# The skip of a chunked recurrence: from four diagonal matmuls on TensorE to a product and a sum on VectorE

## The chip, the cores and the metric

One core of one Trainium2 chip runs the whole kernel. The metric is the device time of one execution in microseconds (us), the median of three runs. A second, profiled execution left the trace from which all rows below are taken.

## What is computed

The reference is a two-layer graph network over N = 4096 nodes of width 256, all in float32. Only the first layer matters here. It adds a graph product to x (4096x4096 weights made from the adjacency matrix by exponentials, times a message matrix), and then a recurrence block:

```
x = x + weights(adj) @ (layernorm(x) @ W + B)
x = x + mamba2(layernorm(x))

# inside mamba2, for 8 heads of 64 channels, t = time step
Y = Y_diag + Y_off + xh * D[:, None]      # D: one number per head, the "skip"
Y = Y * silu(z)
Y = Y * rsqrt(mean(Y * Y)) * norm_w
out = (Y @ W_out) @ W_lin + b_lin
```

`xh * D` is the skip: the convolved input of a channel times its head's D. The second layer (another graph product with a scan, then a mixture of experts) is not touched by the change.

## The kernel before

The 4096 steps are cut into 8 blocks of 512 (`NB`, `TB`), and each block into 4 chunks of 128 steps. The **first stage** of the kernel runs, for every block ib, three streams that are interleaved in one program order per engine: `ssd(ib)` is the recurrence of block ib, `pre_a(ib + 1)` makes the inputs of the next block (norm, projections, convolution, gates), and `product_a(ib + 2)` is the graph product of the block after that. The order is written out as a list (`order_a`, made by `braid`), from which every engine takes its steps. Nothing is scheduled at run time: an engine that waits keeps all that stands behind it waiting too.

Blocks 0 to 5 have a graph product whose weights must be prepared (`product_a`, matmuls of L535). ScalarE takes a logarithm and two exponentials of each tile of `raw`, and VectorE makes two passes over it, L966 and L971 (128x1024 each, two tiles at a time, each with both inputs in SBUF). L535 waits for L971. In blocks 6 and 7 the filling work is the second layer's graph product (L558), whose matrix is used as it is loaded, without preparation.

In a chunk, `inner(s)` turns the chunk's x into rows with four transposes (L610) into a PSUM bank `X`; VectorE makes `xdt` (x times dt, L1066), `bn` (L1069) and `cbm` (L1071) from it; GpSimd makes `rdA` (L1860), `xdec` (L1868, from xdt) and the masked `E` (L1873). `outer(s)` lets TensorE multiply the state h0 (L638, bank `Yo`), make the new state (L643, bank `St`), and sum in bank `Y` first the skip (L648: four 128x128 matmuls with a diagonal matrix of D, `diagD`) and then the in-chunk part (L654: eight matmuls of 64 columns). VectorE takes `tmp` = Yo times a decay (L1082), h0 = hd + St (L1087), tmp += Y (L1091) and z = tmp * z (L1094). GpSimd's `hd` (L1885) decays h0 for the next chunk.

Beside these, the prediction speaks of `xc` (L1011 on VectorE, the last step of pre_a's norm, for which the sixteen small matmuls of L576 wait), of L1049 (the gate's product, behind a tanh on ScalarE), of the transposes L677 behind VectorE's L1104, and of `Wc` (L1132), which is made once in the message stage, the first 45 us, from the matmuls of L712.

Of the kernel before, what the change touches and what calls it, by code (L numbers as in the profile page):

```python
# [9 lines left out]
ALU = mybir.AluOpType  # L10
# [4 lines left out]
NB = N // TB  # L15
# [88 lines left out]
def build(nc, t):  # L104
    with ExitStack() as ctx:
        sems = {}

        def S(name):
            if name not in sems:
                sems[name] = ctx.enter_context(nc.semaphore(name))  # L110
            return sems[name]

        def sb(c, name, shape, dt=F32):
            return c.enter_context(nc.sbuf_tensor(name, shape, dt))
# [28 lines left out]
        diagD = sb(cA, "diagD", [128, 4, 128])  # L143
# [16 lines left out]
        bns = [sb(cA, f"bn{i}", [128, 64]) for i in range(2)]  # L160
        cbm = sb(cA, "cbm", [128, 128])
# [64 lines left out]
        ring_a, ring_b = Ring(PS[2:5], 6 * NB // 2), Ring(PS[5:8], 6 * NB // 2 + 4)  # L226
# [5 lines left out]
        def message_use(ib, i):  # L232
            if ib % 2:
                return ring_b.use(ib // 2 * 6 + (4 if ib > 1 else 0) + i)
            return ring_a.use(ib // 2 * 6 + i)
# [243 lines left out]
        def _(e):  # L479
# [120 lines left out]
            def ssd(ib):  # L600
# [24 lines left out]
                def outer(s):  # L625
# [19 lines left out]
                    w.wait_ge(S("setup"), 7)  # L645
                    w.wait_ge(Y.evac, Y.n - 1)
                    for m in range(4):
                        e.matmul(Y.ps[:, m * 128:(m + 1) * 128], cc[:, m, ts_], diagD[:, m, :], start=m == 0, stop=False,  # L648
                                 skip_group_check=True)
# [3 lines left out]
                    for h in range(8):  # L653
                        i = e.matmul(Y.ps[:, h * 64:(h + 1) * 64], Es[:, h, :], xd[:, h * 64:(h + 1) * 64], start=False,  # L654
                                     stop=h == 7, skip_group_check=True)
# [49 lines left out]
            for i in range(NB // 2):  # L705
                if i == 1:
                    w.wait_ge(S("d_Wo"), 32)
                    for m in range(4):
                        b = combined_use(m)
                        w.wait_ge(b.evac, b.n - 1)  # L710
                        for k in range(2):
                            x = e.matmul(b.ps[:, 0:256], YT[:, k, m * 128:(m + 1) * 128], Wlin[:, k, :],  # L712
                                         start=k == 0, stop=k == 1)
                        x.then_inc(b.full, 1)
                a, b = messages(2 * i), messages(2 * i + 1)
                follow(order_msg[i], a=a, b=b, p=p)
                rest(a)
                rest(b)
# [213 lines left out]
        def _(e):  # L932
# [10 lines left out]
            for m in range(4):  # L943
                e.tensor_scalar(diagD[:, m, :], ident, col("D0", m), None, ALU.mult).then_inc(S("setup"), 1)
# [107 lines left out]
            def ssd(ib):  # L1052
# [3 lines left out]
                def inner(s):  # L1056
# [8 lines left out]
                    w.wait_ge(S("xdec"), c - 1)  # L1065
                    e.tensor_tensor(heads(xd[:, :]), heads(X.ps[:, :]), dt[:, 8 * s:8 * s + 8, None].broadcast_to([128, 8, 64]),  # L1066
# [7 lines left out]
                def outer(s):  # L1074
# [8 lines left out]
                                    ALU.mult).then_inc(Yo.evac, 1)  # L1083
                    yield
# [5 lines left out]
                    w.wait_ge(Yo.evac, Yo.n)  # L1090
# [36 lines left out]
            for i in range(NB // 2):  # L1127
                if i == 1:
                    for m in range(4):
                        b = combined_use(m)  # L1130
                        w.wait_ge(b.full, b.n)
                        e.tensor_scalar(Wc[:, m, :], b.ps[:, 0:256], col("nw", m), None, ALU.mult).then_inc(b.evac, 1)  # L1132
                a, b = messages(2 * i), messages(2 * i + 1)
                follow(order_msg[i], a=a, b=b, p=p)
                rest(a)
                rest(b)
# [863 lines left out]
```

## Time and profile before

| | |
|---|---|
| runs | 2886.9 us median (2885.34 to 2891.23, three runs) |
| profiled execution | 2887.87 us, of which the span of its instructions is 2885.8 us |
| TensorE busy | 2505.6 us (87% of the span) |
| VectorE busy | 2119.0 us (73%) |
| ScalarE, GpSimd busy | 1348.4 us (47%), 961.7 us (33%) |
| mean granted TensorE clock | 0.937 |
| first stage with chunks | about 260 to 1273 us |

Busy time counts a matmul's whole passage through the array, so that a busy TensorE isn't one at its peak. VectorE's 73% is a mean over stages: it is highest in the second layer's scan, behind the stage that is changed.

### The profile page before, as it was taken

The numbers are of one execution on the slowest core, as the hardware profiler recorded it, in microseconds if no ns is written. First come the engines' busy times: TensorE is split into PE (matmuls) and PEld (weight loads), VectorE is DVE, ScalarE is ACT, GpSimd is POOL, SyncE is SP. The second block draws the span as 40 slices with busy tenths as digits, with TensorE's granted clock in tenths as the row PEclk, the third lists the DMA queues.
The fourth block names the chain that finished last, engine by engine and source line by source line (L and its number), as shares of the span: only waits on it lengthen the run. The fifth ranks groups of instructions, "written<-read, shape, count | busy, mean of one in ns | idle before, by whom it ended". The sixth has DMA issues, their size and how long they took to land.

```text
span 2885.8 us, 24290 instructions
## 1 busy us (share of the span) xinstructions
PE 2505.6 (87%) x8262; PEld 1277.1 (44%) x8262; DVE 2119.0 (73%) x2426; ACT 1348.4 (47%) x1935; POOL 961.7 (33%) x723
## 2 busy tenths in 40 slices
PE   7998999999999999988888888888888876765997
PEld 3443444444444444443434343434434343443775
DVE  4665666666667664326999899999999999895564
ACT  4565656565646553214444434434353444552332
POOL 0002232313131313304455554645455464670000
PEclk9998999999999999999999999998999978777999
DMA  4222222222222231123323232322323110102021
GB/s 177 91 88 66 66 83 65 79 71 71 77 73 68 71 104 43 51 83 111 94 83 103 73 109 73 102 80 88 99 84 105 56 50 16 51 31 95 30 66 37
DMA packets 68412, 221.03 MB, mean 77 GB/s; under 512 B 7570, under 2 KB 7826, under 8 KB 67906
## 3 DMA queue, kind: packets, MB, share of 16 engines
q1 hardware_dynamic: 64082, 204.00, 22.4%
q0 software_dynamic: 3664, 14.45, 1.3%
q8 instruction: 66, 1.08, 0.2%
q10 hardware_dynamic: 544, 1.05, 0.1%
q14 instruction: 56, 0.46, 0.1%
HBM read 199.28 MB, written 20.19 MB: 76 GB/s over the span
## 4 chain that ended last, share of the span: by engine, by line
PE 51%; DVE 27%; issue 14%; ACT 6%; POOL 1%; DMA 1%; DVEq 0%; SPq 0%; ACTq 0%; POOLq 0%
PE ps L535 13%; DVE h L1265 9%; DVE acc L1239 7%; PE ps L558 5%; ACT th L1432 2%; PE ps L807 2%; PE ps L654 2%; PE ps L686 2%; PE ps L585 2%; PE ps L587 1%; PE ps L621 1%; PE ps L638 1%; PE ps L643 1%; DVE u L1182 1%; DVE wgt L966 1%
## 5 line engine op out<-in xcount | busy, mean ns | idle before, releaser
L1935 POOL TENSOR_TENSOR dB<-du,bc 128x512 f32<-128x512 f32 x512 | 649.3, 1273 | 559.2 <-DVE h L1265 556.4
L1265 DVE TENSOR_TENSOR_SCAN h<-ps,hst,dB 128x512 f32<-128x512 f32 x512 | 649.3, 1273 | 13.7 <-POOL dB L1935 6.6
L1432 ACT ACTIVATE ps<-dt,cols 128x512 f32<-128x512 f32 x512 | 350.9, 688 | 442.5 <-DVE h L1265 438.3
L535 PE MATMUL ps<-wgt,msg 128*128 128x512 f32 x1024 | 530.7, 621 | 23.0 <-DVE wgt L971 22.6
L558 PE MATMUL ps<-raw,msg 128*128 128x512 f32 x1024 | 543.4, 623 | 3.0 <-DMA msg<-tmp_m 3.0
L807 PE MATMUL ps<-consts,h 128*128 128x128 f32 x2048 | 353.5, 302 | 211.2 <-DVE acc L1239 196.9
L807 PEld LDWEIGHTS ps<-consts,h 128*128 128x128 f32 x2048 | 263.2, 153 | 531.9 <-DVE acc L1239 368.1
L1239 DVE SCALAR_TENSOR_TENSOR acc<-ps,Ct,acc 128x512 f32<-128x512 f32 x450 | 326.7, 726 | 8.9 <-PE ps L807 8.9
L535 PEld LDWEIGHTS ps<-wgt,msg 128*128 128x128 f32 x1024 | 184.2, 194 | 254.8 <-issue 200.7
L1432 ACT ACTIVATE wgt<-wgt 128x1024 f32<-128x1024 f32 x256 | 258.1, 1047 | 38.2 <-DVE wgt L966 35.7
L558 PEld LDWEIGHTS ps<-raw,msg 128*128 128x128 f32 x1024 | 176.5, 199 | 127.8 <-issue 127.0
L966 DVE SCALAR_TENSOR_TENSOR wgt<-wgt 128x1024 f32<-128x1024 f32 x128 | 176.4, 1418 | 69.5 <-ACT wgt L1432 69.5
L971 DVE SCALAR_TENSOR_TENSOR wgt<-raw,wgt 128x1024 f32<-128x1024 f32 x128 | 163.6, 1318 | 17.6 <-ACT wgt L1432 17.3
L1432 ACT ACTIVATE wgt<-raw 128x1024 f32<-128x1024 f32 x128 | 127.8, 1046 | 0.6 <-DMA raw<-in_adjT 0.3
L1430 ACT ACT_TABLE_LOAD x81 | 103.9, 1283 | 43.6 <-DVE u L1182 13.7
L1873 POOL TENSOR_TENSOR E<-E,cbm 128x1024 f32<-128x1024 f32 x32 | 81.6, 2551 | 112.5 <-ACT E L1432 107.1
L1845 POOL COPY xbc<-xbc 128x12 f32<-128x12 f32 x8 | 11.9, 1482 | 318.5 <-DVE cc L1036 318.5
L1036 DVE SCALAR_TENSOR_TENSOR cc<-xbc,cols,cc 128x512 f32<-128x512 f32 (+1 forms) x144 | 112.3, 780 | 3.5
L1901 POOL DMA_DIRECT2D tmp_x<-xb x8 | 5.5, 690 | 288.7 <-DVE xb L1114 288.7
L1868 POOL TENSOR_TENSOR xdec<-xdt,ecd 128x512 f32<-128x512 f32 x32 | 33.3, 1042 | 195.0 <-DVE xdt L1066 195.0
L1433 ACT ACTIVATE tmp<-z 128x512 f32<-128x512 f32 x32 | 20.2, 630 | 167.0 <-DVE z L1094 167.0
L1432 ACT ACTIVATE g<-ps,b 128x512 f32<-128x512 f32 x64 | 42.4, 686 | 111.8 <-PE ps L887 109.3
(273 smaller groups left out, 3682.9 us busy)
## 6 DMA issues: line engine op xcount, KB each, us to landing
raw<-in_adjT SPq DMA_DIRECT2D x256, 512.0 KB, 3.6
bc<-tmp_bc SPq DMA_DIRECT2D x64, 512.0 KB, 4.8
xb<-in_xT POOLq DMA_DIRECT2D x8, 512.0 KB, 4.1
tmp_x<-xb POOLq DMA_DIRECT2D x8, 512.0 KB, 3.1
x<-tmp_x SPq DMA_DIRECT2D x8, 512.0 KB, 4.6
tmp_x<-x SPq DMA_DIRECT2D x8, 512.0 KB, 3.5
tmp_xn<-x SPq DMA_DIRECT2D x8, 512.0 KB, 3.6
raw<-tmp_xn SPq DMA_DIRECT2D x8, 512.0 KB, 4.1
```

The source lines that it names most:

```text
L535: x = e.matmul(P[d][:, :], msg[:, j, d * 128:(d + 1) * 128], wgt[g % NW][:, l, :], start=j == 0, stop=j == NJ - 1)
L558: x = e.matmul(P[d][:, :], msg[:, j, d * 128:(d + 1) * 128], raw[g % 4][:, l, :], start=j == 0, stop=j == NJ - 1)
L807: i = e.transpose(b.ps[:, m * 128:(m + 1) * 128], hr[n % 3][:, m, s * 128:(s + 1) * 128], ident)
L966: e.scalar_tensor_tensor(wgt[i % NW][:, :, :], wgt[i % NW][:, :, :], -2.0, wgt[i % NW][:, :, :], ALU.add, ALU.mult).then_inc(S("q"), 1)
L971: e.scalar_tensor_tensor(wgt[i % NW][:, :, :], raw[i % 4][:, :, :], 1.0, wgt[i % NW][:, :, :], ALU.is_lt, ALU.mult).then_inc(S("wgt"), 1)
L1036: e.scalar_tensor_tensor(c, xbc[0:wd, m, k:k + TB], col("cw0", 4 * m + k)[0:wd, :], c, ALU.mult, ALU.add).then_inc(S("conv"), 1)
L1239: e.scalar_tensor_tensor(acc[:, s, :], b.ps[:, :], c, acc[:, s, :], ALU.mult, ALU.add).then_inc(b.evac, 1)
L1265: e.tensor_tensor_scan(hr[n % 3][:, m, :], PS[4 + k % 2].t[:, :], dBr[k % 4][:, :], hst[:, n % 16, m:m + 1], ALU.mult, ALU.add).then_inc(S ...
L1430: e.preload_act_table_set(need)
L1432: return e.activation(out, in_, func, bias=bias, scale=scale)
L1873: e.tensor_tensor(E[s % 2][:, :, :], E[s % 2][:, :, :], cbm[:, None, :].broadcast_to([128, 8, 128]), ALU.mult).then_inc(S("M"), 1)
L1935: e.tensor_tensor(dBr[k % 4][:, :], du[:, m, :], bcr[i % 3][:, n % 2, :], ALU.mult).then_inc(S("dB"), 1)
```

## The change

The skip leaves TensorE. VectorE multiplies X, while it is in PSUM, by a row of D that stands in all 128 partitions (`Dbc`), into a new buffer `skip`, and adds that to `tmp` later on. The four matmuls of a chunk go. `Dbc` is made once: the four diagonal blocks that `diagD` held are written into `skips[0]`, one matmul with a matrix of ones sums them over the partitions, and VectorE copies the sum out of PSUM.

```
-        diagD = sb(cA, "diagD", [128, 4, 128])
+        Dbc = sb(cA, "Dbc", [128, 512])
...
+        skips = [sb(cA, f"skip{i}", [128, 512]) for i in range(2)]
...
@@ TensorE, outer(s)
-                    w.wait_ge(S("setup"), 7)
                     w.wait_ge(Y.evac, Y.n - 1)
-                    for m in range(4):
-                        e.matmul(Y.ps[:, m * 128:(m + 1) * 128], cc[:, m, ts_], diagD[:, m, :], start=m == 0, stop=False,
-                                 skip_group_check=True)
                     yield
...
-                        i = e.matmul(Y.ps[:, h * 64:(h + 1) * 64], Es[:, h, :], xd[:, h * 64:(h + 1) * 64], start=False,
+                        i = e.matmul(Y.ps[:, h * 64:(h + 1) * 64], Es[:, h, :], xd[:, h * 64:(h + 1) * 64], start=h == 0,
...
@@ TensorE, message stage, behind L712
+                    b = combined_use(4)
+                    w.wait_ge(S("setup"), 7)
+                    w.wait_ge(b.evac, b.n - 1)
+                    e.matmul(b.ps[:, :], one, skips[0][:, :], start=True, stop=True).then_inc(b.full, 1)
...
@@ VectorE, start
-                e.tensor_scalar(diagD[:, m, :], ident, col("D0", m), None, ALU.mult).then_inc(S("setup"), 1)
+                e.tensor_scalar(skips[0][:, m * 128:(m + 1) * 128], ident, col("D0", m), None, ALU.mult).then_inc(S("setup"), 1)
...
@@ VectorE, inner(s)
                     w.wait_ge(S("xdec"), c - 1)
+                    w.wait_ge(combined_use(4).evac, combined_use(4).n)
+                    e.tensor_tensor(skips[s % 2][:, :], X.ps[:, :], Dbc[:, :], ALU.mult).then_inc(S("skip"), 1)
                     e.tensor_tensor(heads(xd[:, :]), heads(X.ps[:, :]), dt[:, 8 * s:8 * s + 8, None].broadcast_to([128, 8, 64]),
                                     ALU.mult).then_inc(X.evac, 1)
...
@@ VectorE, outer(s)
                     e.tensor_tensor(heads(tmp[:, :]), heads(Yo.ps[:, :]), ecd[:, 0, s, :, None].broadcast_to([128, 8, 64]),
                                     ALU.mult).then_inc(Yo.evac, 1)
+                    w.wait_ge(S("skip"), c + 1)
+                    w.wait_ge(Yo.evac, Yo.n)
+                    e.tensor_tensor(tmp[:, :], tmp[:, :], skips[s % 2][:, :], ALU.add).then_inc(S("skipped"), 1)
                     yield
...
                     w.wait_ge(Y.full, Y.n)
-                    w.wait_ge(Yo.evac, Yo.n)
+                    w.wait_ge(S("skipped"), c + 1)
                     e.tensor_tensor(tmp[:, :], tmp[:, :], Y.ps[:, :], ALU.add).then_inc(Y.evac, 1)
...
@@ VectorE, message stage, behind L1132
+                    b = combined_use(4)
+                    w.wait_ge(b.full, b.n)
+                    e.tensor_copy(Dbc[:, :], b.ps[:, :]).then_inc(b.evac, 1)
```

The steps' places in the written order stay, so the two new instructions of a chunk stand directly beside those that they follow. The rows below are the order of the built programs. The first place is VectorE's queue at the start of a block: the first chunk's step, the preparation of weights, the second chunk's step and the norm. Before:

```order
L1066 TENSOR_TENSOR xdt<-ps,sm 128x512
L1069 COPY bn<-ps 128x64
L1071 TENSOR_TENSOR cbm<-ps,consts 128x128
L1008 TENSOR_TENSOR xc<-xb,ps 128x1024
L966 SCALAR_TENSOR_TENSOR wgt<-wgt 128x1024 x2
L1066 TENSOR_TENSOR xdt<-ps,sm 128x512
L1069 COPY bn<-ps 128x64
L1071 TENSOR_TENSOR cbm<-ps,consts 128x128
L1011 TENSOR_TENSOR xc<-xc,rr 128x1024
L971 SCALAR_TENSOR_TENSOR wgt<-raw,wgt 128x1024 x2
```

The same place now (line numbers are those of the changed kernel):

```order
L1068 TENSOR_TENSOR skip<-ps,Dbc 128x512
L1069 TENSOR_TENSOR xdt<-ps,sm 128x512
L1072 COPY bn<-ps 128x64
L1074 TENSOR_TENSOR cbm<-ps,consts 128x128
L1009 TENSOR_TENSOR xc<-xb,ps 128x1024
L967 SCALAR_TENSOR_TENSOR wgt<-wgt 128x1024 x2
L1068 TENSOR_TENSOR skip<-ps,Dbc 128x512
L1069 TENSOR_TENSOR xdt<-ps,sm 128x512
L1072 COPY bn<-ps 128x64
L1074 TENSOR_TENSOR cbm<-ps,consts 128x128
L1012 TENSOR_TENSOR xc<-xc,rr 128x1024
L972 SCALAR_TENSOR_TENSOR wgt<-raw,wgt 128x1024 x2
```

Each chunk's product stands ahead of xdt, and so the second one stands ahead of the norm's last step. The second place is VectorE's queue in the third chunk of a block, from the gate's product to the prepared weights. Before:

```order
L1049 SCALAR_TENSOR_TENSOR cc<-th,cc 128x1024
L966 SCALAR_TENSOR_TENSOR wgt<-wgt 128x1024 x2
L1082 TENSOR_TENSOR tmp<-ps,ecd 128x512
L1087 TENSOR_TENSOR hs<-hd,ps 64x512
L1049 SCALAR_TENSOR_TENSOR z<-sq,z 128x1024
L971 SCALAR_TENSOR_TENSOR wgt<-raw,wgt 128x1024 x2
```

And now:

```order
L1050 SCALAR_TENSOR_TENSOR cc<-th,cc 128x1024
L967 SCALAR_TENSOR_TENSOR wgt<-wgt 128x1024 x2
L1085 TENSOR_TENSOR tmp<-ps,ecd 128x512
L1089 TENSOR_TENSOR tmp<-tmp,skip 128x512
L1093 TENSOR_TENSOR hs<-hd,ps 64x512
L1050 SCALAR_TENSOR_TENSOR z<-sq,z 128x1024
L972 SCALAR_TENSOR_TENSOR wgt<-raw,wgt 128x1024 x2
```

The sum with the skip stands between tmp and the state, ahead of the second pass over the weights.

## Rows read from the trace of the kernel before

**Rows 1.** The page's busy times: us, share of the span, instructions.

```profile
PE 2505.6 (87%) x8262; PEld 1277.1 (44%) x8262; DVE 2119.0 (73%) x2426; ACT 1348.4 (47%) x1935; POOL 961.7 (33%) x723
```

**Rows 2.** Busy time by stretch: PE, PEld, DVE, ACT, POOL, granted clock, DMA.

```profile
547.00:553.00 6.00, 6.00 (x7) 1.29 (x6) 1.96 (x3) 2.58 (x5) 3.92 (x3) 0.51 0.44 137
...
1092.00:1230.00 138.00, 129.71 (x483) 66.47 (x484) 56.01 (x88) 36.60 (x64) 44.76 (x30) 0.99 0.14 42
538.00:674.00 136.00, 131.75 (x411) 61.95 (x410) 91.00 (x105) 81.19 (x105) 35.76 (x22) 0.97 0.23 74
```

**Rows 3.** The chain that ended last, blocks 2 to 4: start, us, what.

```profile
538.03 2.91 DVE wgt L966
540.94 0.60 DVE xdt L1066
...
543.80 1.95 PE ps L576 x16
...
554.13 0.89 PE ps L648 x8
...
599.74 0.88 PE ps L535 x2
...
674.20 2.91 DVE wgt L966
...
811.87 2.91 DVE wgt L966
...
951.26 2.91 DVE wgt L966
```

**Rows 4.** GpSimd and VectorE in time behind L576's release, block 2.

```profile
541.62 1.04 POOL L1868 TENSOR_TENSOR xdec<-xdt,ecd 128x512 f32<-128x512 f32 x1 [1.76 <-DVE xdt L1066]
543.68 3.41 POOL L1873 TENSOR_TENSOR E<-E,cbm 128x1024 f32<-128x1024 f32 x1 [1.02 <-ACT E L1432]
...
541.79 1.95 DVE L1011 TENSOR_TENSOR xc<-xc,rr 128x1024 f32<-128x1024 f32 x1
543.67 1.21 DVE L971 SCALAR_TENSOR_TENSOR wgt<-raw,wgt 128x1024 f32<-128x1024 f32 x1
...
544.80 3.37 DVE L971 SCALAR_TENSOR_TENSOR wgt<-raw,wgt 128x1024 f32<-128x1024 f32 x1
```

**Rows 5.** GpSimd and VectorE in time, third chunk of block 2.

```profile
591.68 2.08 POOL L1885 TENSOR_TENSOR hd<-hs,ecd 64x512 f32<-64x512 f32 x1
597.25 4.23 POOL L1885 TENSOR_TENSOR hd<-hs,ecd 64x512 f32<-64x512 f32 x1 [3.49 <-DVE hs L1087]
...
591.63 1.23 DVE L1049 SCALAR_TENSOR_TENSOR cc<-th,cc 128x1024 f32<-128x1024 f32 x1 [4.32 <-ACT th L1432]
...
592.78 2.07 DVE L966 SCALAR_TENSOR_TENSOR wgt<-wgt 128x1024 f32<-128x1024 f32 x1
...
595.90 0.68 DVE L1082 TENSOR_TENSOR tmp<-ps,ecd 128x512 f32<-128x512 f32 x1
596.50 0.67 DVE L1087 TENSOR_TENSOR hs<-hd,ps 64x512 f32<-64x512 f32 x1
```

**Rows 6.** TensorE's weight loads in block 2 that waited for VectorE.

```profile
565.64 0.30 PEld L535 LDWEIGHTS ps<-wgt,msg 128*128 128x128 f32 x2 [0.83 <-DVE wgt L971]
...
599.49 0.30 PEld L535 LDWEIGHTS ps<-wgt,msg 128*128 128x128 f32 x2 [0.58 <-DVE wgt L971]
613.39 0.42 PEld L677 LDWEIGHTS ps<-consts,z 128*128 128x128 f32 x4 [0.75 <-DVE z L1104]
```

**Rows 7.** VectorE's 128x512 product with both inputs in SBUF, grouped.

```profile
L1094 DVE TENSOR_TENSOR z<-tmp,z 128x512 f32<-128x512 f32 x32 | 23.0, 720 | 1.1
```

**Rows 8.** The chain in block 7, the last skip.

```profile
1227.89 0.89 PE ps L648 x8
```

**Rows 9.** The message stage: the last Wc, and TensorE's first L535.

```profile
38.20 0.48 DVE L1132 TENSOR_SCALAR Wc<-ps,cols 128x256 f32<-128x256 f32 x1 [0.38 <-PE ps L712]
...
42.22 1.22 PE L535 MATMUL ps<-wgt,msg 128*128 128x512 f32 x1 [4.06 <-DVE wgt L971]
```

More of the change, by code:

```diff
@@ L223, in build @@
         lane_b = (ccs[0][:, 2:4, :], ccs[0][:, 4:6, :], th[:, 0, :])
-        ring_a, ring_b = Ring(PS[2:5], 6 * NB // 2), Ring(PS[5:8], 6 * NB // 2 + 4)
+        ring_a, ring_b = Ring(PS[2:5], 6 * NB // 2), Ring(PS[5:8], 6 * NB // 2 + 5)
         prod = [Ring(PS[0:1], 2 * NB + 2), Ring(PS[1:2], 2 * NB)]
@@ L233, in message_use @@
             if ib % 2:
-                return ring_b.use(ib // 2 * 6 + (4 if ib > 1 else 0) + i)
+                return ring_b.use(ib // 2 * 6 + (5 if ib > 1 else 0) + i)
             return ring_a.use(ib // 2 * 6 + i)
```

## The prediction

> **What bounds the kernel now.** The page's busy times [rows 1] come first: TensorE has 87% and VectorE 73% of the span, so work is moved from the busiest engine to the second. Shares over a whole span settle nothing, so the stretches come next [rows 2]. In block 2 (538 to 674 us) TensorE is busy 131.75 of 136 us and VectorE 91.00; in blocks 6 and 7 (1092 to 1230) it is 129.71 of 138 against 56.01. VectorE has room in both. Whether it has room where TensorE waits for it, only the chain of waits tells [rows 3]. It is mostly TensorE, but every block of 0 to 5 begins in the same way: VectorE's L966, then xdt, then the norm's last step (L1011), and only then TensorE's L576. From one L966 to the next is 136.17 us (538.03 to 674.20), 137.67 us, then 139.39 us. Last, I looked at TensorE's weight loads that had to wait [rows 6]: in a block of this kind three of them stand close behind VectorE, at 565.64, 599.49 and 613.39. A block is a sequence of stretches, each bounded by TensorE or by VectorE with next to nothing between them. So I cost the change stretch by stretch.
>
> **What goes, what comes.** A chunk's four diagonal matmuls are one piece of 0.89 us on the chain [rows 3] (eight records of 128 columns take what two of 512 do, 0.88). There are 32 chunks. On VectorE each chunk gains a product and a sum of 128x512. The product reads PSUM and a row, as xdt does, which takes 0.60 us on the chain [rows 3]. It is started back to back, so 0.60 is what it adds. The sum reads two SBUF tiles and waits for the tmp ahead of it; the nearest row is L1094, the same shape with the same kind of wait, 0.72 us [rows 7].
>
> **Blocks 0 to 5.** The five terms, each from the end of the one before, with block 2's times.
>
> *Start of the block, to L576.* The product of the second chunk stands ahead of xdt, on the chain: +0.60. It also moves VectorE against GpSimd. Look at the two engines behind L576 [rows 4]: L971's first pass started at 543.67 and took 1.21, and GpSimd's E asked at 543.68 and took 3.41. The second pass of L971 took 3.37, that is 2.16 longer than the first: it stood still until E was done. So these two engines exclude each other here, and VectorE won by 0.01 us. E hangs on ScalarE and TensorE and stays at 543.68; L1011 and L971 come 0.60 later, at 544.28. E is then the first to ask. Does VectorE keep its place, since L1011 holds it and L971 follows without a gap, or is E let in? Both happen in the third chunk [rows 5]: hd, asked for at 591.68 while L1049 ran, was let in ahead of L966 (2.07 where 1.21 is normal), while hd at 597.25 stood behind three passes of VectorE and took 4.23. In the first case, as in the new one, VectorE's running instruction had itself had to wait for GpSimd (L1011 takes 1.95 with xdec running, and L1049 started while E ran); in the second it had not. I take the first as the nearer. Then E runs from 544.28 for about 2.3, L971's first pass is done near 547.8, and TensorE's L535, which began behind L576 at 545.75 (543.80 and 1.95), begins near 548.1. That is +2.3 in all, 1.7 of it for the lost place. The bounds are +0.6 and +2.3.
>
> In the Trainium skill, "SBUF: State Buffer", section "Who interferes with whom", a VectorE instruction with two SBUF inputs and a GpSimd instruction that reads SBUF lock each other out, and whichever issues first holds the ports for its whole instruction. The trace agrees on the lock (3.37 against 1.21). By its letter E, at 543.68, is ahead of L971, at 544.28, and the sum would take +2.3; but the same rule would have let in hd at 597.25, and it was not let in.
>
> *First skip, to L535 at 565.64.* TensorE loses 0.89. The weights that it waits for there come from L971, which hangs on xdt (on L610's transposes, behind the removed skip). That path also gets 0.89 earlier, but carries the new product: -0.89 + 0.60 = -0.29. The new sum lies in VectorE's wait for L643, over 3 us, and is hidden.
>
> *Second skip.* The path to the next weights runs over L654, L1094 and ScalarE, all of them behind TensorE. The new product comes after these weights and before a wait of 4.32 us for the tanh [rows 5], which covers it; the new sum falls into the wait for L643. -0.89.
>
> *Third skip, to L535 at 599.49.* VectorE has no gap here. From L1049 (591.63) on it runs L966 twice, L1082 (595.90), L1087 (596.50), L1049 again and L971; TensorE's L535 begins at 599.74 [rows 3], 0.25 after the load that waited for L971 [rows 6]. The two paths from the tanh are equal, so TensorE's 0.89 gains nothing, and the sum's 0.72 is added: +0.72. What would cover it is a VectorE that had been idle, and it isn't.
>
> *Fourth skip, to L677.* L677 waited for L1104 [rows 6], which hangs on L1094, L1433 and ScalarE from the weights of 599.49 on. TensorE arrives 0.89 earlier and waits: 0. The last sum lies ahead of a wait for ScalarE.
>
> One block: 2.3 - 0.29 - 0.89 + 0.72 = +1.84. Six blocks: +11.0.
>
> **Blocks 6 and 7.** No weights are prepared, VectorE is idle 60% of the time [rows 2], and all eight skips stand on the chain as TensorE's own (the last one in block 7 [rows 8]). The product and the sum fall into VectorE's waits. 8 x -0.89 = -7.1.
>
> **Message stage.** VectorE's L966 starts at once behind the last Wc (38.20), and TensorE's L535 waited 4.06 us for what follows from it [rows 9]. Now one more matmul (0.88) and one more copy (about 0.6) come before L966, less 0.4 that lay between Wc and L966: +1.1.
>
> **Sum.** 11.0 - 7.1 + 1.1 = +5.0 us. The profiled execution took 2887.87 us with a span of 2885.8, 1.0 above the median of the runs. On the median: 2886.9 + 5.0 = 2891.9, so 2892. A measurement of this kernel tells about 0.2%, 5.8 us, from no change: 2881.1 to 2892.7.
>
> **The rivals.**
> - *VectorE keeps its place before E.* The second hd speaks for it [rows 5]. The block's first term is +0.60, a block +0.14, and the sum 0.8 - 7.1 + 1.1 = -5.2: 2881.7. It ends on the other side, and what decides is whether L971, arriving 0.6 us behind E's request, still starts first. Chance 0.25, of which 0.10 beyond the bound.
> - *TensorE alone is the bound.* If L535's waits were absorbed, all 32 skips would pay: -28.5 + 1.1, 2859.5. Against it stand the three loads that waited [rows 6]. Chance 0.07.
> - *The clock.* Between 547 and 553 TensorE was granted 0.51 of its clock [rows 2], so the 1.2 GHz level, right behind the small matmuls of L576 and the wait for L1011. The change makes that wait longer, and adds one of some 1.6 us at 599. The blocks of 139.39 us have more of it than that of 136.17 us [rows 3]: 3.2 us each. If three more blocks get this, or the stretch gets longer, 5 to 10 us come on top: 2897 to 2902. Against it: how the spells fall differs from block to block already, and they can also get fewer. Chance 0.17.
> - *The change doesn't do what it says.* The program's order shows the matmuls gone and both instructions in place, so this is out.
>
> **How the numbers follow.** My forecast has 0.48, within 2886 to 2898, the spread being the clock's; it lies so close to the bound that I give half of it to slower and half to no difference. With the rivals: faster 0.10 + 0.07 and some for fewer slow spells, 0.20; same 0.24 + 0.14 = 0.38; slower 0.24 + 0.17 and a remainder, 0.42. The range leaves out the bound by TensorE alone and the far end of the clock: 2875 to 2904.
>
> **What the profile after would show.** Right: in blocks 0 to 5 E takes about 2.4 us at that place and no longer 3.41, L971's first pass takes over 3 us, and L535 behind L576 waits for it; the load at the third skip waits some 1.6 us more; the period of a block is near 138 us where it was 136.17; 1092 to 1230 is 7 us shorter. Wrong: E still takes over 3.4 us there (then 2882), the period falls by 3 us (then TensorE alone), or granted clocks in blocks differ by more than the sum. The step that I trust least is E's turn, 10 us of the sum; next the clock.

## The result, and the profile after

The changed kernel took 2903.4 us median (2899.17 to 2904.93, six runs) against 2889.4 us (2885.34 to 2891.23, six runs) for the kernel before on the same chip. The ratio is 1.0048, with a 95% interval of 1.0035 to 1.0060: it is slower by 0.48%, +14.0 us, where +5 us was forecast. The time lies in the range, 0.6 us under its upper end, and outside the stretch that I gave my own case (2886 to 2898).

The page's busy times of the changed kernel, to be held against [rows 1]:

```profile
PE 2501.1 (86%) x8008; PEld 1259.8 (43%) x8008; DVE 2193.0 (76%) x2491; ACT 1348.4 (46%) x1935; POOL 959.8 (33%) x723
```

TensorE has 254 instructions fewer and only 4.5 us less busy time, although the skips alone were 32 x 0.89 = 28.5 us. The rest ran at a lower clock (0.929 on the mean of the span, 0.937 before). The same stretches as in [rows 2], counted from the start of the span, so that the last one lies some 15 us earlier in the work than it did before (columns: PE, PEld, DVE, ACT, POOL, granted clock, DMA):

```profile
547.00:553.00 6.00, 5.18 (x19) 3.58 (x20) 6.00 (x3) 1.35 (x2) 6.00 (x3) 0.60 0.23 60
...
538.00:674.00 136.00, 127.78 (x371) 58.62 (x370) 100.82 (x112) 78.48 (x102) 34.97 (x21) 0.95 0.23 74
1092.00:1230.00 138.00, 125.85 (x373) 58.89 (x372) 66.59 (x96) 39.41 (x65) 44.61 (x29) 0.90 0.17 58
```

VectorE counts as busy for all 6 us behind the norm's last step (1.96 before), most of it in passes that stand still, as the rows below show. In the last two blocks the granted clock is 0.90 where it was 0.99. The chain in block 2, which answers to [rows 3]; the block begins 2.90 us later than it did:

```profile
540.93 2.91 DVE wgt L967
543.84 0.60 DVE skip L1068
544.44 0.56 DVE xdt L1069
...
545.37 1.88 DVE xc L1012
547.24 3.31 DVE wgt L972
...
550.59 2.08 PE ps L536 x2
```

The product stands on the chain with its 0.60, and then a new link: L972, the second pass over the weights, 3.31 us. The two engines in time at this place, as in [rows 4]:

```profile
546.59 2.87 POOL L1882 TENSOR_TENSOR E<-E,cbm 128x1024 f32<-128x1024 f32 x1 [0.43 <-ACT E L1441]
549.42 2.02 POOL L1894 TENSOR_TENSOR hd<-hs,ecd 64x512 f32<-64x512 f32 x1
...
547.16 3.38 DVE L972 SCALAR_TENSOR_TENSOR wgt<-raw,wgt 128x1024 f32<-128x1024 f32 x1
...
550.46 3.91 DVE L972 SCALAR_TENSOR_TENSOR wgt<-raw,wgt 128x1024 f32<-128x1024 f32 x1
```

E is now ahead (2.87 us, 3.41 before) and VectorE's first pass takes 3.38 us instead of 1.21. TensorE's loads that waited, as in [rows 6]; the first is new:

```profile
550.59 0.50 PEld L536 LDWEIGHTS ps<-wgt,msg 128*128 128x128 f32 x2 [0.62 <-DVE wgt L972]
...
570.85 0.30 PEld L536 LDWEIGHTS ps<-wgt,msg 128*128 128x128 f32 x2 [1.43 <-DVE wgt L972]
...
604.60 0.30 PEld L536 LDWEIGHTS ps<-wgt,msg 128*128 128x128 f32 x2 [2.27 <-DVE wgt L972]
...
618.50 0.42 PEld L674 LDWEIGHTS ps<-consts,z 128*128 128x128 f32 x4 [1.64 <-DVE z L1110]
```

From the anchor (538.03 before, 540.93 now) the last three come 2.31, 2.21 and 2.21 us later than before.

**The clock at a block's end.** The last wait of blocks 0 to 4, and of the stretch ahead of block 0, is for VectorE's xb (L996; L997 now). The chain from there, first in the kernel before, at the end of block 2:

```profile
661.34 0.69 DVE xb L996
...
662.71 1.10 PE ps L487 x2
663.81 0.44 PE ps L610 x4
...
664.73 1.05 PE ps L489 x2
665.78 1.72 PE ps L535 x4
```

And in the changed kernel:

```profile
666.43 0.69 DVE xb L997
...
667.82 2.05 PE ps L488 x2
669.86 0.85 PE ps L611 x4
...
671.39 1.06 PE ps L490 x2
672.44 1.72 PE ps L536 x4
```

The same matmuls behind the same wait take twice as long (0.44 and 0.85): they run at 1.2 GHz and not at 2.4 (granted clock 0.50 between 667.82 and 670.71, and 1.00 between 662.71 and 664.25 in the kernel before). From the first of them to the next block's 128x1024 subtraction (L1008, L1009 now) it is 3.1 us in the first case and 4.7 in the second. I call this stretch the tail of the block. Of the six tails behind such a wait two were of the short kind before, and none is in this trace. Block 5 has no such wait, and its tail takes 3.1 us in both.

I count a block from one of these subtractions to the next; block 0 begins with the second. There are eight subtractions, and the last begins at 1077.4 us before and at 1092.7 us now:

```profile
L1008 DVE TENSOR_TENSOR xc<-xb,ps x8: 1220/1222/1222, 152.1 to 1077.4; 128x1024 f32<-128x1024 f32 x8
```

```profile
L1009 DVE TENSOR_TENSOR xc<-xb,ps x8: 1220/1220/1222, 151.7 to 1092.7; 128x1024 f32<-128x1024 f32 x8
```

Up to there the two executions differ by +15.3 us. From there to the end of the span they take 1808.4 and 1808.9 us, +0.5, where 7.1 less was forecast. This rest holds blocks 6 and 7 and also some 1650 us of stages that the change doesn't touch. Blocks 6 and 7 by themselves, from the eighth subtraction to the last product of tmp and z (L1094; L1100 now), end here:

```profile
L1094 DVE TENSOR_TENSOR z<-tmp,z x32: 691/692/821, 284.5 to 1231.3; 128x512 f32<-128x512 f32 x32
```

```profile
L1100 DVE TENSOR_TENSOR z<-tmp,z x32: 691/692/822, 283.2 to 1249.3; 128x512 f32<-128x512 f32 x32
```

That is 153.9 us before and 156.6 now.

### The profile page after: what moved, and what is told of

It reads as the page before. It is cut to its first block, busy times and chain, and to the rows that moved or that the text cites. A ratio compares the mean times of both kernels' runs of the same rounds, so it can differ in the third digit from the quotient of the medians.

```text
span 2901.6 us, 23888 instructions
## 1 busy us (share of the span) xinstructions
PE 2501.1 (86%) x8008; PEld 1259.8 (43%) x8008; DVE 2193.0 (76%) x2491; ACT 1348.4 (46%) x1935; POOL 959.8 (33%) x723
## 4 chain that ended last, share of the span: by engine, by line
PE 46%; DVE 30%; issue 14%; ACT 7%; POOL 1%; DMA 1%; DVEq 0%; SPq 0%; ACTq 0%; POOLq 0%
PE ps L536 11%; DVE h L1274 9%; DVE acc L1248 7%; PE ps L559 5%; ACT th L1441 2%; DVE wgt L972 2%; PE ps L808 2%; DVE wgt L967 2%; PE ps L683 2%; PE ps L622 1%; ACT wgt L1441 1%; PE ps L651 1%; PE ps L588 1%; DVE u L1191 1%; PE ps L586 1%
## 5 line engine op out<-in xcount | busy, mean ns | idle before, releaser
L536 PE MATMUL ps<-wgt,msg 128*128 128x512 f32 x1024 | 530.4, 624 | 39.8 <-DVE wgt L972 39.4
L536 PEld LDWEIGHTS ps<-wgt,msg 128*128 128x128 f32 x1024 | 186.6, 195 | 286.4 <-issue 213.1
L967 DVE SCALAR_TENSOR_TENSOR wgt<-wgt 128x1024 f32<-128x1024 f32 x128 | 174.1, 1400 | 65.8 <-ACT wgt L1441 65.8
L972 DVE SCALAR_TENSOR_TENSOR wgt<-raw,wgt 128x1024 f32<-128x1024 f32 x128 | 179.8, 1445 | 17.6 <-ACT wgt L1441 17.2
L1441 ACT ACTIVATE E<-ps 128x512 f32<-128x512 f32 x64 | 38.1, 595 | 121.6 <-PE ps L622 121.5
```

The costliest lines, as they stand in the source:

```text
L536: x = e.matmul(P[d][:, :], msg[:, j, d * 128:(d + 1) * 128], wgt[g % NW][:, l, :], start=j == 0, stop=j == NJ - 1)
L967: e.scalar_tensor_tensor(wgt[i % NW][:, :, :], wgt[i % NW][:, :, :], -2.0, wgt[i % NW][:, :, :], ALU.add, ALU.mult).then_inc(S("q"), 1)
L972: e.scalar_tensor_tensor(wgt[i % NW][:, :, :], raw[i % 4][:, :, :], 1.0, wgt[i % NW][:, :, :], ALU.is_lt, ALU.mult).then_inc(S("wgt"), 1)
L1441: return e.activation(out, in_, func, bias=bias, scale=scale)
```

## The experiments

All ratios are to the kernel before, run on the same chip. "To the 8th" is the start of the eighth subtraction in the profiled execution (the message stage, the stretch up to block 0, and blocks 0 to 5), and "0 to 5" the part of it from the second subtraction on, the six blocks alone. "Rest" is what follows up to the end of the span, and "6, 7" the part of it that is blocks 6 and 7, up to the start of the last L1094. "Block" is the time from the fourth subtraction (529.6 before) to the first matmul behind the block's last wait, so without the tail. In "product, no sum" and "late and held" this block had an additional stretch at half clock; the next two of "late and held" took 133.20 us. The median and the ratio are of the timed runs, the other columns of one traced execution each. The labels that end in 2 stand for edits whose first run gave no time.

| kernel | median us | ratio (95%) | to the 8th | 0 to 5 | rest | 6, 7 | block |
|---|---|---|---|---|---|---|---|
| before | 2889.4 | 1 | 1077.4 | 823.3 | 1808.4 | 153.9 | 133.07 |
| after | 2903.4 | 1.0048 (1.0035 to 1.0060) | 1092.7 | 841.9 | 1808.9 | 156.6 | 135.27 |
| one-column copy | 2902.2 | 1.0041 (1.0027 to 1.0054) | 1090.6 | 835.8 | 1813.0 | 160.9 | 135.68 |
| no skip at all | 2869.4 | 0.9935 (0.9921 to 0.9948) | 1068.4 | 814.3 | 1803.9 | 148.8 | 131.24 |
| product, no sum | 2892.3 | 1.0014 (1.0005 to 1.0023) | 1089.4 | 835.1 | 1803.5 | 148.6 | 135.02 |
| sum, no product | 2876.6 | 0.9960 (0.9946 to 0.9974) | 1071.8 | 818.4 | 1805.4 | 151.6 | 131.97 |
| after, E held | 2890.9 | 1.0016 (1.0007 to 1.0025) | 1081.2 | 826.2 | 1808.8 | 156.6 | 133.27 |
| before, E held | 2887.0 | 0.9995 (0.9986 to 1.0004) | 1077.5 | 823.3 | 1805.0 | 153.8 | 133.07 |
| product late | 2893.3 | 1.0023 (1.0014 to 1.0032) | 1089.7 | 835.7 | 1802.9 | 148.1 | 135.41 |
| late and held | 2879.3 | 0.9975 (0.9962 to 0.9988) | 1075.6 | 822.0 | 1802.0 | 148.2 | 134.32 |
| two products behind, held | 2876.3 | 0.9961 (0.9947 to 0.9974) | 1064.0 | 812.9 | 1803.4 | 148.5 | 132.02 |

**One column copied** (`tiny`), the kernel before with

```
+                    e.tensor_copy(nudge[:, :], X.ps[:, 0:1]).then_inc(S("nudge"), 1)
                     e.tensor_tensor(heads(xd[:, :]), heads(X.ps[:, :]), dt[:, 8 * s:8 * s + 8, None].broadcast_to([128, 8, 64]),
                                    ALU.mult).then_inc(X.evac, 1)
```

> The kernel before, all of its computation kept, with one more VectorE instruction in each of the 32 chunks: a copy of one column (128x1) from the bank of X, issued between the wait on X and the xdt multiplication, where the changed kernel has its product. It asks whether the delay at the start of a block comes from the product's own 0.6 us or from VectorE losing its place to GpSimd's E. Theory of the hand-over: the small copy is enough for VectorE's first wgt multiplication to come after GpSimd's E has begun; the load of TensorE that waits for wgt starts about 1.7 to 1.9 us later in each of blocks 0 to 5, so 6 x 1.8 = about +11 us (+9 to +13), and in the trace E stands ahead of the wgt multiplication. Rival, sum of durations: each copy costs its own 0.06 to 0.1 us, at most 32 x 0.1 = 3 us, and likely under +1 us, since only the first chunk's copy of a block lies on the path.

Measured: ratio 1.0041, so 12 us, and 14 by the medians (2888.2 for the kernel before beside it). The chunk that the expectation calls a block's first is the one that the prediction counts as its second. The two engines at the start of block 2:

```profile
545.25 0.15 DVE L1067 COPY nudge<-ps 128x1 f32<-128x1 f32 x1
...
546.24 1.95 DVE L1012 TENSOR_TENSOR xc<-xc,rr 128x1024 f32<-128x1024 f32 x1
548.11 3.39 DVE L972 SCALAR_TENSOR_TENSOR wgt<-raw,wgt 128x1024 f32<-128x1024 f32 x1
...
548.07 2.35 POOL L1875 TENSOR_TENSOR E<-E,cbm 128x1024 f32<-128x1024 f32 x1 [0.96 <-ACT E L1434]
...
551.55 0.50 PEld L536 LDWEIGHTS ps<-wgt,msg 128*128 128x128 f32 x2 [1.45 <-DVE wgt L972]
```

The copy adds 0.07 us to the chain. That is enough: L972 asks at 548.11, 0.04 after E, where it was 0.01 ahead of it [rows 4], and takes 3.39 us. TensorE's load waits 1.45 us. Counted from the subtraction, L536 begins 1.41 us later and the block is 2.61 us longer; the difference is half clock, since the matmuls behind the wait stayed at 1.2 GHz for longer. Over the six blocks it makes +12.5 us. Two of them (the two that were 1.6 us longer before, by a slow stretch of their own) grew by only 0.7. Blocks 6 and 7, which prepare no weights, took 7.0 us more in this execution, at a granted clock of 0.94 where it was 0.99; it was the longest of the five. The hand-over is shown; the sum of durations, under 1 us, is refuted.

**No skip at all** (`mm_only`), the kernel before without

```
-                    for m in range(4):
-                        e.matmul(Y.ps[:, m * 128:(m + 1) * 128], cc[:, m, ts_], diagD[:, m, :], start=m == 0, stop=False,
-                                 skip_group_check=True)
```

> The kernel before with its 128 diagonal matmuls left out and nothing put in their place, so the skip D*x is missing from the output. It prices what the change gave back. By the terms of the prediction: per block of 0 to 5 the first skip about -0.3 to -0.9 us and the second -0.89, the third and the fourth 0 (VectorE sets the end there), in blocks 6 and 7 eight times -0.89 = -7.1; in sum -14 to -18 us, about 2872 us. Rival, TensorE alone the bound: all 32 chunks pay 0.89, -28.5 us, about 2861. Rival, the clock: the granted clock falls more often once TensorE has these gaps, and blocks 6 and 7 give back less than 3 us of their 7.1, as in the changed kernel's trace, in sum -8 to -12 us.

Measured: 18.8 us less (2888.2 for the kernel before beside it), a little more than the 14 to 18 expected. In a block the chain is 1.83 us shorter (133.07 to 131.24), just the sum of -0.94 at the first skip and -0.89 at the second, with nothing at the third and fourth. So VectorE, for which the loads wait there, sets the end of the third and fourth chunk, and TensorE is not alone the bound. Of blocks 6 and 7, 5.1 us came back, not 7.1. And of 1.83 per block not all stays: this block's tail took 4.4 us where it was 3.1, and the six blocks together are 9.0 us shorter. The traced execution was the longest of the five, 4.8 us above their median, so the trace doesn't show all of the 18.8.

**The product without the sum** (`no_sum`), the changed kernel with

```
-                    e.tensor_tensor(tmp[:, :], tmp[:, :], skips[s % 2][:, :], ALU.add).then_inc(S("skipped"), 1)
```

> The changed kernel without the second half of its work: the product with the row is made in each chunk, the addition to tmp is not (the skip is missing from the output). Against the changed kernel: if the addition's price sits in the third chunk of blocks 0 to 5 only (0.8 us there, hidden elsewhere), the time falls by 6 x 0.8 = 5 us (4 to 7, the third skip paying nothing more), to about 2898 us, still above the kernel before by about 9 us. Rival, all 32 additions count: 32 x 0.79 = 25 us less. Rival, the addition is hidden everywhere: no change.

**The sum without the product** (`no_product`), the changed kernel with

```
-                    e.tensor_tensor(skips[s % 2][:, :], X.ps[:, :], Dbc[:, :], ALU.mult).then_inc(S("skip"), 1)
-                    e.tensor_tensor(tmp[:, :], tmp[:, :], skips[s % 2][:, :], ALU.add).then_inc(S("skipped"), 1)
+                    e.tensor_tensor(tmp[:, :], tmp[:, :], Dbc[:, :], ALU.add).then_inc(S("skipped"), 1)
```

> The changed kernel without the product with X: the addition stays and adds the spread row Dbc itself (the skip is wrong by the factor x). Against the changed kernel: the load that waits for wgt at the start of a block comes 2.2 us earlier as in the kernel before, with VectorE's wgt multiplication ahead of GpSimd's E again, and the first chunk's xdt 0.6 earlier: 6 x (2.2 to 2.9) = 13 to 17 us less, about 2888 us, and so about the time of the kernel before or 1 to 5 us below it. Rival, the sum of durations: only 0.6 us in a block, 4 to 7 us less, about 2898 us.

Measured: without the sum +0.14%, so 0.34% under the changed kernel, about 10 us, where 5 was expected. The trace confirms the place: in block 2 it is 6.59 us from the gate's product (L1050) to the pass L972 at the third skip, where the changed kernel has 7.39 and the kernel before 6.60, so the sum makes 0.8. The further 5 us are not assigned. The traced executions are 8.7 us apart, 5.4 of it in the rest, but two later executions of the changed kernel differ from its first by 3.2 and 5.8 us there with nothing changed. Without the product the time is 0.40% under the kernel before, so 0.88% or 25 us under the changed one, where 13 to 17 was expected. Its block shows the sum by itself: 131.97 against 131.24 without any skip, +0.73, in place of the 0.72 of the prediction. The product thus makes 3.3 of the changed kernel's 135.27: 1.9 at the start (L536 behind L577), 0.6 ahead of the next xdt, and 0.8 that the clock adds. Blocks 0 to 5 took 818.4 us without the product, 18 to 23 less than in three executions of the changed kernel, so most of the 25 lies where it was expected. Both expectations had the place right and were too small. The clock is the part that block 2 shows; how much of the 10 and 25 us it makes in the timed runs is not shown.

**E held back** (`hold_e2`), the changed kernel with one wait on GpSimd ahead of E:

```
+                    if s == 1 and ib < 6:
+                        w.wait_ge(S("wgt"), 36 + 16 * ib)
                     e.tensor_tensor(E[s % 2][:, :, :], E[s % 2][:, :, :], cbm[:, None, :].broadcast_to([128, 8, 128]),
                                    ALU.mult).then_inc(S("M"), 1)
```

> The changed kernel, all of it, with one more wait: in the chunk beside the anchor of blocks 0 to 5 GpSimd begins its multiplication of E only when VectorE has done the two wgt multiplications that follow there. The order of the kernel before (VectorE ahead of E) is so restored by a semaphore, while the product stays where it is. Theory of the hand-over: the first wgt multiplication takes about 1.2 us again and TensorE's load waits for it no more; of the 2.2 us that a block lost at its start 1.6 come back and the product's 0.6 stays: 6 x 1.6 = about -10 us against the changed kernel (-8 to -13), about 2893 us. Rival, E is what counts: E ends some 2 us later and the Y matmuls, which wait for it, take the delay over: no gain or a loss.

**The same wait in the kernel before** (`before_hold2`).

> The kernel before, all of it, with the same wait of GpSimd's E for VectorE's two wgt multiplications. A control: in the kernel before TensorE's load did not wait for wgt there, so an earlier wgt should be worth nothing: within 1 to 2 us of the kernel before. Were it 5 us or more faster, the wait and not the skip would be what the held versions gain by.

Measured: by the ratios 0.32% or 9 us under the changed kernel, as expected, and no difference from before in the control. In block 2:

```profile
544.55 1.21 DVE L972 SCALAR_TENSOR_TENSOR wgt<-raw,wgt 128x1024 f32<-128x1024 f32 x1
...
547.07 2.35 POOL L1884 TENSOR_TENSOR E<-E,cbm 128x1024 f32<-128x1024 f32 x1 [3.52 <-DVE wgt L972]
549.38 1.04 POOL L1896 TENSOR_TENSOR hd<-hs,ecd 64x512 f32<-64x512 f32 x1
```

L972 takes 1.21 us again, E 2.35 and hd 1.04 (2.02 in the changed kernel). The block is 133.27, +0.20 over before. The prediction's terms with the start at its lower bound make that: 0.60 - 0.29 - 0.89 + 0.72 + 0 = +0.14. What a late E could cost does not show.

**The product late** (`late2`), in the chunk beside the anchor of blocks 0 to 5 only: xdt signals a semaphore of its own, and the product follows the norm's last step.

```
                 e.tensor_tensor(xc[:, :, :], xc[:, :, :], two(rr), ALU.mult).then_inc(S("xn"), 1)
+                while later:
+                    later.pop()()
...
+                    product = lambda: e.tensor_tensor(skips[s % 2][:, :], X.ps[:, :], Dbc[:, :], ALU.mult)
...
+                    if late(ib, s):
+                        later.append(lambda: product().then_inc(X.evac, 1))
```

> The changed kernel, all of it, with the product of the chunk beside the anchor of blocks 0 to 5 moved from ahead of xdt to behind the xc multiplication that TensorE waits for. So xdt, the cbm multiplication and the xc multiplication come 0.6 us earlier, as in the kernel before, but the product now stands just ahead of the wgt multiplications, and E is ready by then. Theory of the hand-over: E is let in between them as with the one-column copy, the load waits for wgt as before, and the start of a block still costs 2.2 to 2.6 us: within 3 us of the changed kernel (2900 to 2906). Rival, the place of the product on the path is what costs: 6 x 2.2 = 13 us less, about 2890 us.

**Late and held** (`late_hold2`): this and the wait of E.

> Both edits together: the product behind the xc multiplication and E held until the two wgt multiplications are done. All of the computation is kept. By the terms measured so far the start of a block costs nothing now; what is left against the kernel without product and without sum (2869.4 us) is the addition's 7 us and the product's 0.6 us ahead of the second xdt on the path in each of blocks 0 to 5 (4 us): 2880 to 2884 us, 4 to 8 us under the kernel before. If it stays above 2886 us, another cost of the product is still missing from the account.

Measured: late alone 2893.3 us, 0.25% under the changed kernel, so neither theory's number by the time. The trace separates the parts. In block 2:

```profile
546.90 0.68 DVE L1078 TENSOR_TENSOR skip<-ps,Dbc 128x512 f32<-128x512 f32 x1
547.50 2.85 DVE L980 SCALAR_TENSOR_TENSOR wgt<-raw,wgt 128x1024 f32<-128x1024 f32 x1
...
546.90 2.36 POOL L1902 TENSOR_TENSOR E<-E,cbm 128x1024 f32<-128x1024 f32 x1 [1.01 <-ACT E L1458]
```

The product is off the path to xc, E is let in behind it all the same, the pass over the weights takes 2.85 us, and the block is 135.41, +2.34. So the hand-over stands. Blocks 0 to 5 took 835.7 us, where three executions of the changed kernel have 841.9, 837.2 and 836.3, so against the shortest of them late gains under 1 us there. The rest took 1802.9, where those three have 1808.9, 1803.1 and 1805.7. A gain of 7 us by the ratios is thus more than the place of the product explains; its source is not resolved. With the wait as well it is 2879.3 us, 0.25% under the kernel before, 0.7 us below the stretch expected, and all of the computation is kept.

**Two products behind the weights** (`behind`): as the last, and the product of the next chunk (the one ahead of xdt at 566.18 in the changed kernel) is made behind the pair of L972.

> All of the computation, from the kernel with the product behind the xc multiplication and E held (2879.3 us): in blocks 0 to 5 the product of the next chunk, which stood ahead of an xdt on the path, now comes behind the pair of wgt multiplications that follow it. The second product's term of the account (0.60 us in each of six blocks) should come back: about -3.6 us, 2874 to 2877 us, so 11 to 14 us under the kernel before. What then stands between it and the kernel without product and without sum (2869.4 us) is the addition alone. Rival, the clock: one tail of a block at half clock costs 1.6 us, and with a few more of them nothing of the 3.6 us is seen.

Measured: 2876.3 us, 11.5 us or 0.39% under the kernel before, as expected. The block is 132.02, where the sum without the product had 131.97: the products cost nothing any more in this block. The 3.0 us between this and the last version are less than the two intervals, so that step rests on the trace, and of its five executions the traced one was the shortest. By its median it is the fastest of the versions that compute everything.

**The clock, looked at again** (`after_again`, `before_again`, `after_timed`: the two kernels unchanged).

> The changed kernel once more, unchanged, for its clock. Theory that the clock is set by the schedule: in each of blocks 0 to 5 the stretch from the load after the block's last wait to the next block's subtraction takes 4.6 to 4.8 us again (it took 3.1 us in two of the six of the kernel before), and the granted clock in the last two blocks is 0.91 again. Rival, it differs from execution to execution: some of these stretches take 3.1 us, or the last blocks show 0.98.

> The kernel before once more, unchanged, for its clock. Theory that the clock is set by the schedule: the stretches at the end of the second and the third block take 3.1 us again and the others 4.5 to 4.7 us, and the last two blocks run at a granted clock of 0.98 to 0.99. Rival, it differs from execution to execution: other blocks are the short ones, or there are more or fewer of them.

> The changed kernel a third time, unchanged, now also timed in five rounds, for the spread that the clock gives it. If its clock differs from execution to execution, the times lie between 2892 and 2906 us, wider than the kernel before on the same chip (2885 to 2891), and the median stays 10 to 15 us above it. If the one execution of 2894 us was an outlier, the times stand together at 2899 to 2905 us.

Measured: in its traces the kernel before repeats itself. The six blocks took 139.38, 136.16, 136.18, 137.67, 139.39 and 134.52 us in the first trace and 139.38, 136.17, 136.19, 137.66, 139.40 and 134.52 in the second, and the rest 1808.4 in both; the 2.2 us between the two spans lie ahead of block 0. Its timed runs are less alike, 2881.8 to 2890.0 in the last nine. The changed kernel doesn't repeat itself: 141.79, 139.90, 139.93, 142.17, 140.52, 137.56 in the first; 140.05, 140.62, 139.27, 140.61, 139.28, 137.39 in the second; all between 139.8 and 140.0 but for the last in the third. Three of the six tails behind a wait for xb, those of blocks 0, 2 and 4, took 3.1 us in the second execution, none in the first and third. Its last two blocks, in the first and in the second execution:

```profile
1093.00:1243.00 150.00, 138.16 (x424) 65.94 (x425) 72.68 (x105) 41.33 (x69) 51.99 (x34) 0.91 0.16 55
```

```profile
1089.00:1239.00 150.00, 136.77 (x450) 65.16 (x451) 75.81 (x111) 41.97 (x71) 52.23 (x34) 0.97 0.17 59
```

At a granted clock of 0.91 the rest takes 1808.9 us, at 0.97 1803.1. So each of my two theories holds for one of the kernels. The timed set gave 2900.1 us (2896.66 to 2900.74) and a ratio of 1.0046 (1.0033 to 1.0060), which repeats the result; the single execution of 2894.1 us is lower than both sets. The last expectation is met in part: the times lie between 2892 and 2906 us and the median 14.4 us above the kernel before, but they lie within 4.1 us, closer together than the kernel before (8.2 us), and they begin 2.3 us below the stretch that I gave for an outlier.

## Why the prediction was right or wrong

The direction was right, and so was the mechanism at the start of a block. The size was 9 us too small, and it would have been further off had misses of both signs not partly cancelled. The steps by the trace of block 2, counted from the anchor:

- *Start of the block.* Forecast +2.3. L536 behind L577 begins 9.66 us behind the anchor, where it was 7.72 (545.75, as the prediction had it): +1.94. The choice between the bounds was right, E was let in; `tiny` shows it without the product, and `hold_e2` takes all but the product's 0.6 back. The reason that I gave for the choice, that VectorE's running instruction had itself waited, was not tested: no run has E ask first behind one that hadn't. An argument from two rows came out right. Then the clock adds: the two matmuls of L536 there took 1.44 us before and 2.08 now, another +0.64.
- *First skip.* Forecast -0.29, and from 1.94 + 0.64 = +2.58 to +2.31 at the load of 570.85 it is -0.27. In `hold_e2` too (+0.29 there in all, where 0.60 - 0.29 = 0.31 was due).
- *Second skip.* Forecast -0.89, measured -0.89 (+2.31 to +1.42).
- *Third skip.* Forecast +0.72, measured +0.79 (+1.42 to +2.21), and +0.73 between `mm_only` and `no_product`. VectorE sets the end here, which `mm_only` confirms from the other side.
- *Fourth skip.* 0, as forecast (+2.21 at L674 too).
- *A block* was to cost +1.84 and cost +2.20, the difference being the half clock behind the new wait (0.64), less 0.36 that the start was overestimated by, and 0.07 of the third.
- *Message stage.* Forecast +1.1, measured +0.7 at its end: the first L536 begins at 42.91 where it was 42.22 [rows 9], yet the last Wc came 0.37 earlier in that execution (37.83, was 38.20). From this Wc to L967's start it is 1.47 us where it was 0.40, so the term was right at +1.07:

```profile
38.69 0.69 DVE L1141 COPY Dbc<-ps 128x512 f32<-128x512 f32 x1 [0.37 <-PE ps L715]
39.30 1.22 DVE L967 SCALAR_TENSOR_TENSOR wgt<-wgt 128x1024 f32<-128x1024 f32 x1
...
42.91 1.12 PE L536 MATMUL ps<-wgt,msg 128*128 128x512 f32 x1 [4.26 <-DVE wgt L972]
```

- *From there to block 0.* Put at nothing. From the last Wc to the first subtraction it is 113.9 us in the first trace of the kernel before and in all three of the changed kernel, and 1.0 us less in the second trace of the kernel before: against the first one the message stage's +1.07 was gone by then, against the second it was there. Behind the L535 of 42.22 [rows 9] the first one stayed at half clock for longer (7.29 us from there to the next L535, 6.25 in the second, at granted clocks of 0.62 and 0.73, and 6.26 in the changed kernel). From the first subtraction to the second it is 102.0 us in both traces of the kernel before, and 99.1, 99.8 and 102.0 in the changed one, at a granted clock of 0.90 before and 0.93, 0.92 and 0.90 now. On the mean block 0 begins 0.8 us earlier than before, where +1.1 was forecast.
- *Blocks 6 and 7.* Forecast -7.1. This is the term that was mis-sized most. They took 153.9 us in both traces of the kernel before, at a granted clock of 0.99, and 156.6, 150.0 and 153.4 in the changed kernel at 0.91, 0.97 and 0.93: -0.5 on the mean. The new work is not the reason, since in these two blocks `late2` is the same code as the changed kernel and took 148.1 us at 0.98 (-5.8), while `mm_only`, with no new work on VectorE at all, took 148.8 at 0.98 (-5.1). An estimate from these rows, time multiplied by granted clock, gives 152 us before and 143 to 145 in the changed kernel, 7 to 9 less: by this estimate the gain of 7.1 was there, and the clock took it back.
- *The stages behind* were put at nothing, and took 1654.5 us before and 1652.3, 1653.0 and 1652.3 now: -2.0 on the mean, in code that is the same. The kernel before with E held, the same code there too, has 1651.1, so a difference of this size needs no change of that code.

In sum: three traces of the changed kernel end on the mean at 2896.5, two of the kernel before at 2884.7, +11.8 us, where +5.0 was forecast. Up to block 0 it is -0.8 (+1.1 forecast), in blocks 0 to 5 +15.1 (+11.0), in blocks 6 and 7 -0.5 (-7.1), behind them -2.0 (0). So the two terms on which the sum rests were 4.1 and 6.6 us too low, and 3.9 us that I had not foreseen came back elsewhere. Of the 4.1, some 2.6 are inside the blocks, by the half clock behind the new wait, and 1.5 in their tails. Of the signs that I named as right, E took 2.87 us and not about 2.4, the load at the third skip waited 1.7 us more as forecast, the period was 139.9 and not 138, and the last blocks weren't 7 us shorter. So the rival "the clock" came true on top of the forecast case: I priced it as another outcome, with a chance of its own, and not as a part of each outcome, though it moved the start of a block, the tails and blocks 6 and 7. Taken from the kernel before, +14.0 us is what that rival priced (10 to 15 us), and the forecast's own case ended at +11. The medians differ by 14.0 and 14.4 us, 2 us more than the traces; what these have in addition is not resolved, since a timed run leaves no trace.

The rival that VectorE keeps its place was wrong for the changed kernel and describes `hold_e2` well. The two hand-overs of [rows 5] pointed to opposite sides; the one that I took as nearer was.

Why the clock falls more often in one schedule than in another, and why the kernel before repeats its pattern in the traces while the changed one doesn't, stays open. I can show what it costs, and not what would keep it up.

## What to carry to other kernels

An instruction added ahead of a place where two engines ask for the same thing within 0.01 us can cost the hand-over and not its own duration: 0.07 us of copying cost some 12 us. Look for such near ties around any insertion, and fix the order by a semaphore if it matters. Put new VectorE work behind the piece that another engine waits for, not ahead of it: the same two products cost 3.3 us in block 2 ahead of that piece and nothing behind it. And where TensorE's removed work leaves it waiting longer, take part of the gain off for the clock: here blocks 6 and 7 gave back 0.5 of 7.1 us on the mean, between -2.7 and +3.9 in three executions of one kernel. A single trace is not enough to read such a term from.

## What the runs showed of the hardware

- The lock between VectorE and GpSimd depends on VectorE's operands. The product (PSUM and a row) ran in its usual 0.68 us from the very moment at which E began (546.90), and E took its usual 2.36, while the pass behind it, with two inputs in SBUF, took 2.85 instead of 1.21. In the Trainium skill, "SBUF: State Buffer", section "Who interferes with whom", a VectorE instruction with at most one SBUF input does not contend with GpSimd outside the 2-port modes, one with two contends with a GpSimd instruction that reads SBUF, and the blocked side stops fully. The trace agrees on the three. The sum reads two SBUF tiles, so by the same rule it can be caught: it took 1.88 us at 550.94 in the held version, beside rdA, and was hidden there.
- VectorE's second pass at the start of a block (550.46, 3.91 us) stood behind two GpSimd instructions in a row: hd, and rdA, which ran from 551.41 for 1.88 us. Once the first pass had come in between E and hd, these two ran back to back. In the held version hd took 1.04 us and not 2.02.
- The same matmuls behind the same wait (L487, L610) take 1.10 and 0.44 us or 2.04 and 0.85. The tail of a block had few lengths, 3.1 us or 4.4 to 4.7 in all of blocks 0 to 5 of all kernels, so that two versions can be compared by blocks with tails of the same kind.
